# A causal mask in the first layer, moved from TensorE products to one VectorE pass

## The reference

```
qkv = xn @ attn_w.T + attn_b                      # per head: q, k, v of 8 columns
mask = arange(n)[:, None] <= arange(n)[None, :]   # key position <= query position
scores = einsum('bhki,bhqi->bhkq', k, q) / sqrt(8)
scores = where(mask, scores, -10000.0)
probs = softmax(scores, axis=2)                   # over the keys
out = einsum('bhkq,bhkl->bhql', probs, v) @ out_w.T + out_b
```

## Time and profile before

| what | value |
|---|---|
| median of 3 runs | 1325.0 us (1321.04 to 1330.04) |
| the profiled execution | 1330.59 us, its span 1328.9 us |
| mean granted TensorE clock | 0.978 |
| PE, DVE, ACT, POOL busy | 1286.8, 982.7, 828.7, 744.0 us |
| instructions | 23542 |

### The profile page before, as it was taken

One profiled execution on the slowest core, in us unless ns is written; L12 is line 12 of the kernel. 1 busy time (PEld: TensorE's weight loads), 2 busy tenths in 40 slices (PEclk: granted clock), 3 DMA queues, 4 the chain that ended last, 5 costly groups with the idle time before them and its releaser, 6 DMA issues.

```text
span 1328.9 us, 23542 instructions
## 1 busy us (share of the span) xinstructions
PE 1286.8 (97%) x8338; PEld 773.1 (58%) x8346; DVE 982.7 (74%) x2344; ACT 828.7 (62%) x1235; POOL 744.0 (56%) x889
## 2 busy tenths in 40 slices
PE   8899999999999999999999999999999999999998
PEld 5444445455544445666666666666666666666666
DVE  4666776877776667777777877877877878878775
ACT  2456576666667655666657666666666666656653
POOL 6154465646555445765655655655655665665553
PEclk9889999999999889999999999999999999999999
DMA  6223233424253141111221120020020120010002
GB/s 191 70 75 94 89 99 105 127 91 130 90 165 108 50 142 38 46 41 45 62 66 45 54 74 21 30 74 21 30 74 21 31 74 21 30 50 22 26 30 74
DMA packets 57751, 90.61 MB, mean 68 GB/s; under 512 B 12315, under 2 KB 23616, under 8 KB 57634
## 3 DMA queue, kind: packets, MB, share of 16 engines
q1 hardware_dynamic: 56482, 88.58, 21.4%
q10 hardware_dynamic: 1152, 0.52, 0.1%
HBM read 43.66 MB, written 44.30 MB: 66 GB/s over the span
## 4 chain that ended last, share of the span: by engine, by line
PE 56%; DVE 2%; ACT 2%; POOL 1%; issue 0%; DVEq 0%
PE bank L1674 7%; PE bank_pair L130 6%; PE bank_pair L155 6%; PE bank_pair L1663 4%; PE bank L1663 4%; PE bank L1675 4%; PE bank L1676 4%; PE bank_pair L1664 4%; PE bank_pair L1665 4%; PE bank L1665 4%; PE bank L1664 4%; PE bank_pair L137 1%; DVE bank_pair L165 1%; DVE a_h L1485 1%; DVE a_h L1491 1%; PE bank_pair L1633 1%
## 5 line engine op out<-in xcount | busy, mean ns | idle before, releaser
L1299 POOL TENSOR_TENSOR a_h_lo<-a_h,a_h_hi 128x512 fp32r<-128x512 f32 x256 | 329.8, 1288 | 129.7 <-ACT a_h_hi L1397 125.4
L189 POOL TENSOR_SCALAR_AFFINE_SELECT E<-E 128x256 f32<-128x256 f32 (+1 forms) x384 | 195.5, 512 | 354.0 <-ACT E L1405 199.3
L689 DVE TENSOR_REDUCE mx<-bank_pair 128x2 f32<-128x1024 f32 (+3 forms) x264 | 209.6, 818 | 119.5 <-PE bank_pair L939 118.1
L1485 DVE SCALAR_TENSOR_TENSOR a_h<-a_h,bank_pair 128x512 f32<-128x512 f32 x256 | 175.5, 686 | 122.1 <-ACT a_h L1393 121.4
L1405 ACT ACTIVATE E<-bank_pair 128x1024 f32<-128x1024 f32 (+1 forms) x192 | 169.8, 884 | 116.3 <-PE bank_pair L137 116.3
L165 DVE CUSTOM_DVE_ANT_0 bank_pair<-bank_pair,mask 128x512 f32<-128x512 f32 x496 | 230.3, 516 | 0.0
L1397 ACT ACTIVATE a_h_hi<-a_h 128x512 fp32r<-128x512 f32 x256 | 161.6, 631 | 86.9 <-DVE a_h L1491 86.9
L779 ACT ACTIVATE E<-bank_pair 128x1024 f32<-128x1024 f32 (+1 forms) x192 | 168.4, 878 | 74.2 <-PE bank_pair L137 72.8
L130 PE MATMUL bank_pair<-st 24*128 24x512 f32 (+3 forms) x1024 | 200.2, 390 | 13.4 <-ACT E L779 4.0
L1393 ACT ACTIVATE a_h<-bank_pair 128x512 f32<-128x512 f32 x256 | 152.1, 594 | 73.3 <-PE bank_pair L1665 70.9
L1491 DVE TENSOR_TENSOR a_h<-a_h,bank 128x512 f32<-128x512 f32 x256 | 175.9, 687 | 26.7
(11 more groups left out here) (209 smaller groups left out, 2278.9 us busy)
## 6 DMA issues: line engine op xcount, KB each, us to landing
st<-stack_d SPq DMA_DIRECT2D x256, 96.0 KB
o_d<-O SPq DMA_DIRECT2D x63, 256.0 KB, 2.1
stack_d<-l_q_k_hi SPq DMA_DIRECT2D x56, 256.0 KB, 3.1
stack_d<-l_q_k_lo SPq DMA_DIRECT2D x28, 256.0 KB, 3.4
st<-ms SPq DMA_DIRECT2D x128, 8.0 KB
wst<-wg_in SPq DMA_DIRECT2D x8, 256.0 KB, 3.2
wst<-wu_in SPq DMA_DIRECT2D x8, 256.0 KB, 3.8
wst<-wd_in SPq DMA_DIRECT2D x8, 256.0 KB, 4.4
```

The costliest lines, as they stand in the source:

```text
L189: return nc.gpsimd.affine_select(out=part, in_=part, compare_op=ALU.is_ge, fill=0.0, base=0, pattern=pattern, channel_multiplier=-1)
L689: ins = nc.vector.tensor_reduce(out, pair[:, :, col:col + width(kb)], AX.X, ALU.max)
L1299: nc.gpsimd.tensor_tensor(h_lo[:, q % RH, :], h[:, q % RH, :], h_hi[:, q % RH, :].bitcast(F32), ALU.subtract).then_inc(h_lo_ready, 1)
L1485: nc.vector.scalar_tensor_tensor(hq, hq, 1.0, g_bank[:, :], ALU.add, ALU.mult).then_inc(silu_ready, 1)
```

## The change

In layer 0, `maxima_of` on DVE calls the helper `maxima` that layer 1 uses, once for each half; and `scores_and_keys` on PE issues each score matmul as a group of its own and no mask products. S_ready is raised by the last score matmul in place of the last mask product. The fillers, the order of both engines and everything in layer 1 stay.

```diff
@@ DVE, maxima_of
                 pair, j = pair_of("S", g, n), n // 3
-                for kb, col in UNITS[n % 3]:
-                    t = NT - 1 - kb
-                    out = mx[:, g % 2, t, :].rearrange("p (r j) -> p r j", j=PLANES)[:, :, j]
-                    ins = nc.vector.tensor_reduce(out, pair[:, :, col:col + width(kb)], AX.X, ALU.max)
+                for r in range(HALVES):
+                    ins = maxima(nc, pair[:, r, :], mask, mx, g, n % 3, r, j)
                 ins.then_inc(S_used, 1)
@@ PE, scores_and_keys
                     for r in range(HALVES):
                         if more and k < len(score_blocks):
-                            scores(nc, pair_of("S", g + 1, n)[:, r, :], stacks[(g + 1) % STACKS], r, n // 3, score_blocks[k], k == 0, False)
+                            ins = scores(nc, pair_of("S", g + 1, n)[:, r, :], stacks[(g + 1) % STACKS], r, n // 3, score_blocks[k], True, True)
                 if more:
-                    for r in range(HALVES):
-                        tiles = pair_of("S", g + 1, n)[:, r, :].rearrange("p (a c) -> p a c", c=P)
-                        diagonal = (tiles[:, 3:4, :], tiles[:, 0:4:3, :], tiles[:, 1:2, :])[n % 3]
-                        part = mask[:, N - P:N].unsqueeze(1).to_broadcast([P, len(score_blocks), P])
-                        ins = nc.tensor.matmul(diagonal, identb[:, :], part, start=False, stop=True)
                     ins.then_inc(S_ready, 1)
```

## The result

The change made the kernel slightly slower: 1327.3 us median of 20 runs (1319.7 to 1341.9) against 1321.4 us of 20 runs of the kernel before (1318.4 to 1330.0), a ratio of 1.0038 with a 95% interval of 1.002 to 1.0056. The forecast was 9 us faster. The ratios leave out runs more than 1.5% above the fastest of the same kernel: two of these 20, and a single one of the kernel before, at 6228 us, among the later ones. The profiled execution took 1321.25 us, its span 1319.5 us at a mean clock of 0.974; the profiled execution of before had 1330.6 us at 0.978. That pair alone looks like a gain of 9 us, and it is not representative: 61 other runs of the kernel before, made beside the experiments, lie between 1318.6 and 1328.9 us at clocks from 0.981 to 0.993 (mean 0.989).

The account below looks back on a forecast made before the run. PE and DVE were taken to be near their limits in turn in layer 0. 12 us saved less 3 us for the clock gave -9 us on 1325.0, so 1316 us; 8-in-10 range 1294 to 1344.

Parts of the forecast that it names:

- The mechanism forecast for the work: Layer 0 quads: earlier PE work net of DVE's longer pass, 1.5 us a batch, 12 us less over 8.25 batches.
- its 31 us: PE in layer 0: most it can gain without the mask products, 0.95 us a quad by start distances, 33 quads.
- its 34: DVE in layer 0: the masked pass by halves and key blocks costs 1.04 us more a quad, 34 us in all.
- the bound by summed durations: DVE in layer 0: if accumulator reads did not lie beside the next pass, 3.3 us more a quad.
- Unit 5's slack of 0.71 us: DVE's idle time before unit 5 in u = 0 quads, said to cover its arrival there 0.5 us later.
- C: The waits move: PE spends its saving waiting for maxima or exponentials; 1325 us, chance 0.20.
- D: DVE becomes the bound in units 1 to 4 of u = 0 and 1: 18 us slower, 1343 us, chance 0.14.
- B: PE is the bound throughout and gains its 31 us, DVE's longer pass hidden in idle time; 1294 us, chance 0.16.
- the clock term: Layer 0: PE's lighter work assumed to put 12 us more at the low clock level, costing 3 us.
- 0.26: Price in us of each microsecond at 1.2 GHz, from u = 3 quads: 14.05 us at clock 1.00, 16.71 at 0.69.
- rival E: The clock falls: less PE activity, longer stays at 1.2 GHz in layer 0; +15 us, 1340 us, chance 0.14.
- its threshold of 100 us more: Layer 0: about 100 us more at 1.2 GHz than now was said to make the kernel 1% slower.

Follow-up runs that it names:

- E2: Kernel before without the mask products, plain maximum over both halves kept, mask left out of the maximum: 1317.0 us, ratio 0.9967.
- E3: Kernel before with mask products kept and DVE's masked pass on top, so the mask is added twice: 1341.3 us, ratio 1.0142.
- E9: Kernel before with four more fillers a quad, one in each gap, mask products kept: 1331.0 us, ratio 1.0079.
- E6: Changed kernel with four more fillers a quad, one in each gap: 1320.8 us, ratio 0.9992.
- E5: Kernel before with four fillers of 512 columns fewer in each quad, mask products and DVE untouched: 1341.7 us, ratio 1.0167.
- E8: Changed kernel with the mask products issued again ahead of each unit's scores, which overwrite them: 1390.6 us, ratio 1.0527.

## Why the prediction was wrong

The mechanism forecast for the work held nearly to the number. I had 0 for u = 0, 0.6 for u = 1, 0.35 for u = 2 and 0.55 for u = 3, together 1.5 us a batch and 12 us in all; the clean steps show 0.17, 0.56, 0.27 and 0.44, together 1.44, u = 2 being good to a few tenths only. E2 and E3 show the two halves: the removal saves 18 of its 31 us, the addition costs 7 of its 34. The sum of the 32 steps in the two profiles, whose clocks happen to be close (51 and 56 us at the low level in them), went from 465.0 to 453.2 us, 11.8 less. DVE's price by start distance (its rows give 6.96 - 5.88 = 1.08 us a quad, not 1.04, a slip without weight) and PE's (0.95, from the start distances alone) came from the right rows, too: the bound by summed durations, 3.3 us a quad, would have put DVE's busy time in 405 us some 90 us up, and it rose by 33. Unit 5's slack of 0.71 us was used up, as said, without making u = 0 longer. Rivals C and D are out: the saving arose, and no kind of step grew. So is B: even without DVE's longer pass (E2) only 18 of the 31 us arise at full clock.

**The step that failed is the clock term**, "so I assume 12 us more at the low level: +3 us". It was mis-sized twice. The extra time at 1.2 GHz was 54 us (83 against 29), more than four times as much, and each of them cost more than 0.26. Up to 54 us by the line of the kernel before (0.27) and from there to 83 by that of the changed kernel (0.43) it makes 19 us. Less the 12 saved that is 7 us slower, and so far apart are the means of the two sets of runs (1321.6 and 1328.8 us).

The 12 us stand on no row: the prediction takes them from "0.95 us less to do" without a step between. The 0.26 is a reading error. It sets the u = 3 step of the earlier trace rows against an ordinary u = 3 step, but the step of the earlier trace rows lies in the last batch but one of layer 0 and has less to do (DVE 9.21 us and 18 instructions in the earlier trace rows, 10.92 and 22 in the earlier trace rows). E9, with the same DVE code, has this step at full clock:

```profile
436.78:449.84 13.06, 12.63 (x114) 6.99 (x111) 9.80 (x18) 7.44 (x11) 6.81 (x9) 1.00 0.22 74
```

That is 1.3 us shorter than E9's ordinary 14.35; in E3 the difference is 0.8 us (13.50 against 14.32), in E6 0.9 us. An estimate from these for the kernel before is 12.8 to 13.2 us, and the price then comes to 0.34 to 0.38 us, close to the 0.37 to 0.39 of the like steps above. With it alone the forecast would still have been 8 us faster; the amount is what decided.

What came true is rival E, to which I gave 0.14, in a milder form: its threshold of 100 us more wasn't reached, nor its sign, a layer-0 clock under 0.9 (the profile has 0.95), and its price was too low. The base was taken from one trace, too. The profiled execution has 59 us at the low level over its span (2 x 0.022 x 1329) where 61 runs average 29. That execution, at 1330.6 us, also lay above all three runs shown, and I noted its distance to the median without asking whether the clock explained it. Last, the 1316 us of the forecast start from the median of three runs, 1325.0; that of 20 is 1321.4.

The removal alone lets 44 us more fall to the low level, the addition alone 26, both 54 to 56: two causes, less work on PE and, as I read E3, a longer wait for others, and not simply additive. That less work is enough by itself, E5 shows in the kernel before; that the loss lies in the clock and not in the waits, E6 with E9. The Trainium skill ("TensorE: Matmul & The Clock Gate", Part 1) says that the slow clock is the default and activity releases it; E5 and E6 agree, with 0.959 and 0.986 for fewer and more fillers. I had cited this beside rival E and then weighed it by three clean steps.

What stays open: the line through each kernel's runs has its own slope (0.27 for before, 0.25 for E9, 0.33 to 0.48 for the others), so the split of the few last microseconds between clock and work is not settled; nor is why E3 is 4 us above its two terms. Which u = 1 steps fall and which stay clean, the waits in PE's timeline don't tell.

## What to carry to other kernels

On a TensorE that fillers keep at speed, taking matmuls away is not a gain until the clock is checked: run the lighter kernel several times, plot time against granted clock, and compare steps at clock 1.00 apart from the share of low time. Take the clock of the baseline from many runs, never from the one profile. Take the price of low-clock time from two steps with the same instruction counts. And give some of the removed activity back as fillers before judging such a change; here that turned a loss of 6 to 9 us into a tie.

## What was not expected of the hardware

- Matmuls of 24 and 26 rows, each on its own 32 of the operand stack's partitions, run side by side, four of 512 columns in 0.44 us, and with a 128-row product between them they no longer do: 1.6 to 2.3 us a quad with what the product itself takes (E8's clean steps are 13.63, 16.95, 16.96 and 15.91 us).
- At clock 1.00 the u = 0 steps repeat within some 0.02 us between batches and runs (11.58 to 11.60 us in twelve clean steps of two profiles of the changed kernel), so that a single clean one measures a change of 0.2 us; u = 1 and 2 scatter by tenths. The scatter of the totals of the changed kernel is nearly all clock: its 26 runs lie within 3.1 us of their line.
- The masked pass beats its looks: one instruction a half and block with its accumulator read costs 0.25 us for 128 columns and 0.61 to 0.65 for 512 from start to start, since the read lies beside the next pass.
